# Experts: the next tokens' transposes ahead of a slice's gate product, and the down weights' split in two

## What is computed

```
scores = softmax(x @ W_router)
topk_vals, topk_idx = top_k(scores, 2)
h = silu(einsum('td,edh->eth', xf, We_gate)) * einsum('td,edh->eth', xf, We_up)
y_all = einsum('eth,ehd->etd', h, We_down)
routed = einsum('etd,te->td', y_all, combine)
```

## Time and profile before

| | us |
|---|---|
| median of 3 runs | 1090.07 (1089.99 to 1092.28) |
| the profiled execution | 1088.47 |
| its span, first to last instruction | 1086.8 |
| TensorE busy | 1016.1 (93%) |
| TensorE weight loads busy | 858.2 (79%) |
| VectorE busy | 666.1 (61%) |
| ScalarE busy | 456.7 (42%) |
| GpSimd busy | 275.8 (25%) |

### The profile page before, as it was taken

The page is one execution under the profiler, slowest core; times in us unless marked ns, Lnnn a source line. Parts: engine busy times, 40 slices in busy tenths (PEclk is TensorE's granted clock), DMA queues, the critical chain, the costliest instruction groups (busy, mean ns, idle before and its releaser), DMA issues. The chain is left out here.

```text
span 1086.8 us, 18081 instructions
## 1 busy us (share of the span) xinstructions
PE 1016.1 (93%) x6368; PEld 858.2 (79%) x6368; DVE 666.1 (61%) x1502; ACT 456.7 (42%) x798; POOL 275.8 (25%) x367
## 2 busy tenths in 40 slices
PE   7899999999979999999859979999999999899997
PEld 5688888888778888887637768888998889778785
DVE  4836556477265776776444847776777776253576
ACT  5623314145125544454443226555655664221110
POOL 4510100213143323333343122212231220503040
PEclk9999999999978999999998979999999999999999
DMA  5403032023877888884432157787778773615042
GB/s 168 180 1 116 0 115 87 0 81 126 205 187 194 212 228 239 218 219 131 171 99 81 63 179 225 252 256 266 243 246 277 251 244 113 213 40 188 6 155 77
DMA packets 87183, 172.66 MB, mean 159 GB/s; under 512 B 8112, under 2 KB 36016, under 8 KB 85328
## 3 DMA queue, kind: packets, MB, share of 16 engines
q1 hardware_dynamic: 81008, 150.08, 44.6%
q0 software_dynamic: 6112, 21.76, 6.1%
HBM read 130.92 MB, written 37.49 MB: 155 GB/s over the span
## 5 line engine op out<-in xcount | busy, mean ns | idle before, releaser
L45 PE MATMUL e_ps_h<-e_x_lo,e_gu_hi 128*128 128x256 f32 (+1 forms) x384 | 111.3, 290 | 10.8 <-DVE e_x_lo L2141 8.7
L45 PE MATMUL a_ps_proj<-region_a_rounded,arena 128*128 128x512 f32 x272 | 107.4, 395 | 11.2 <-DVE region_a_rounded L369 6.2
L953 DVE CUSTOM_DVE_ANT_0 b_dump<-b_ps_s,b_mask 128x128 f32<-128x128 f32 (+1 forms) x256 | 80.4, 354 | 46.5 <-PE b_ps_s L1143 43.3
L47 PE MATMUL e_ps_h<-e_x_hi,e_gu_hi 128*128 128x256 f32 (+1 forms) x384 | 108.2, 282 | 0.0
L46 PE MATMUL e_ps_h<-e_x_hi,e_gu_lo 128*128 128x256 f32 (+1 forms) x384 | 108.2, 282 | 0.0
L46 PE MATMUL a_ps_proj<-region_a_rounded,arena 128*128 128x512 f32 x272 | 106.4, 391 | 0.0
L47 PE MATMUL a_ps_proj<-region_a_rounded,arena 128*128 128x512 f32 x272 | 106.4, 391 | 0.0
L2147 DVE TENSOR_TENSOR e_gu_lo<-f_region_a,e_gu_hi 128x704 fp32r<-128x704 f32 x92 | 81.3, 889 | 26.8 <-ACT e_gu_hi L2057 26.3
L388 DVE SCALAR_TENSOR_TENSOR f_region_b<-a_ps_proj,a_taps,f_region_b 128x510 f32<-128x510 f32 (+2 forms) x96 | 71.7, 746 | 40.8 <-ACT f_region_b L328 38.5
L843 ACT ACTIVATE b_pt<-b_ps_x 128x384 f32<-128x384 f32 x128 | 61.8, 487 | 61.2 <-PE b_ps_x L1167 61.1
L757 POOL TENSOR_SCALAR_AFFINE_SELECT b_pt<-b_pt 128x256 f32<-128x256 f32 x128 | 51.8, 407 | 122.6 <-ACT b_pt L843 121.9
(11 more groups left out here) (400 smaller groups left out, 2693.7 us busy)
## 6 DMA issues: line engine op xcount, KB each, us to landing
f_region_a<-we_gate_up SPq DMA_DIRECT2D x88, 352.0 KB, 5.6
qk_split<-arena SPq DMA_DIRECT2D x24, 512.0 KB, 5.8
y_slots<-f_region_b SPq DMA_DIRECT2D x16, 512.0 KB, 3.4
f_x_next<-x SPq DMA_DIRECT2D x7, 1024.0 KB, 7.1
b_sk<-qk_split SPq DMA_DIRECT2D x24, 256.0 KB, 4.4
b_sq<-qk_split SPq DMA_DIRECT2D x24, 256.0 KB, 5.7
f_region_a<-we_down SPq DMA_DIRECT2D x12, 512.0 KB, 4.0
f_region_b<-we_down SPq DMA_DIRECT2D x11, 512.0 KB, 4.0
```

The lines of the kernel that those rows point to most:

```text
L45: pe.matmul(out, a_hi, b_lo, start=first, stop=False)
L47: return pe.matmul(out, a_hi, b_hi, start=False, stop=last)
L953: ins = dve.tensor_tensor_reduce(dump[:, n % 2, cols], ps_s[:, n % 2, cols], mask[:, cols], -1.0, 3e38, ALU.add, ALU.min, peak[:, u, k, i: ...
```

## The change

TensorE: in a small tile `turn(m, k + 1)` stands ahead of both products of the slice, not between them. ScalarE and VectorE: the next tile's tokens are split at the second tile's end, behind its output copy; the third part of the next tile's gate and up moves behind them. In the small tile the first third of the down weights (unit 0) is split at the start, ahead of the fourth part, and the other two thirds after the silu (ScalarE) or after the small hidden product (VectorE). Nothing that SP and POOL do is reordered.

```diff
-            def split_down(m, k):
-                act.wait_ge(dn_loaded[k % 2], 32 * (SPAN * m + (k + 1) // 2))
-                act.wait_ge(y_ready, count(m, k, BLOCKS, 1))
-                act.activation(dn_hi[:], dn_raw[k % 2], ACT.Copy).then_inc(dn_hi_done, 1)
+            def split_down(m, k, units=slice(0, U)):
+                if units.start == 0:
+                    act.wait_ge(dn_loaded[k % 2], 32 * (SPAN * m + (k + 1) // 2))
+                    act.wait_ge(y_ready, count(m, k, BLOCKS, 1))
+                act.activation(dn_hi[:, units], dn_raw[k % 2][:, units], ACT.Copy).then_inc(dn_hi_done, 1)
@@ ScalarE, large_tile
                 if k % SPAN == 1:
-                    for c in range(3):
-                        split_gate_up(m, k + 2, c)
+                    split_gate_up(m, k + 2, 0)
+                    split_gate_up(m, k + 2, 1)
                 output(m, k)
+                if k % SPAN == 1:
+                    split_x(m, k + 2)
+                    split_gate_up(m, k + 2, 2)
@@ ScalarE, small_tile
-                split_down(m, k)
+                split_down(m, k, slice(0, 1))
                 split_gate_up(m, k + 1, 3)
                 act.wait_ge(h_ready, U * number(m, k) + 1)
                 act.activation(small_sg, bank(0), ACT.Silu).then_inc(silu_done, 1)
-                split_x(m, k + 1)
+                split_down(m, k, slice(1, U))
                 act.wait_ge(h_ready, U * number(m, k) + 3)
@@ VectorE
-            def split_down(m, k):
-                dve.wait_ge(dn_hi_done, number(m, k) + 1)
-                dve.tensor_tensor(dn_lo[:], dn_raw[k % 2], dn_hi[:].bitcast(F32), ALU.subtract).then_inc(dn_lo_done, 1)
+            def split_down(m, k, units=slice(0, U)):
+                dve.wait_ge(dn_hi_done, count(m, k, 1, 2) + (1 if units.start == 0 else 2))
+                ins = dve.tensor_tensor(dn_lo[:, units], dn_raw[k % 2][:, units], dn_hi[:, units].bitcast(F32), ALU.subtract)
+                if units.stop == U:
+                    ins.then_inc(dn_lo_done, 1)
@@ VectorE, large_tile: as ScalarE's
@@ TensorE, small_tile
+                turn(m, k + 1)
                 small_hidden(m, k, 0)
-                turn(m, k + 1)
                 small_hidden(m, k, 1)
```

## The result

| | before | after |
|---|---|---|
| median of the timed runs, us | 1089.01 (1084.41 to 1095.32, 16 runs) | 1083.32 (1079.34 to 1088.36, 16 runs) |
| ratio of the times, 95% interval | | 0.9946 [0.9927, 0.9965] |
| profiled execution, us | 1088.47 | 1080.20 |
| its span, us | 1086.8 | 1078.4 |

The interval stands for 3.8 to 7.9 us, so rival (a) with its 7.5 us lies inside it too; (b), (c), (d) and (e) lie outside. A second set of runs gave 0.9943 [0.9915, 0.997]. Single executions lie up to 11 us apart before and 9 us after, so one profiled pair doesn't measure the gain: its spans differ by 8.4 us.

A forecast was written before the change was run, and what follows sets the result against it. TensorE bounds the kernel, with 9.4 us of waits at seven small tiles set by ScalarE's order and the third part. Place gains of 5.8, rounded to 5.7, gave 1090.07 - 5.7 = 1084.4 us; range 1081.5 to 1088.0 (8 in 10).

The forecast's parts named there:

- (a): Rival, chance 0.10: ScalarE's chain is shorter, TensorE's queue sets all restarts but for gathers; gain 7.5 us, 1082.6 us.
- (b): Rival, chance 0.11: later store and earlier gather each cost 0.5 us in seven places; 2.2 us gain left, 1087.9.
- (c): Rival: gate and up loads land at fixed times, only the first place gains; 1089.0 us; chance 0.09 together with (e).
- (d): Rival, chance 0.06: TensorE stands at later-landing gathers ahead of both products; 2.2 us later each loses 6.0 us, 1096.1 us.
- (e): Rival: no effect, something else comes last at the same moment; 1090 us; chance 0.09 together with (c).
- The chain of before: ScalarE's output copy through down weights, fourth part, silu and tokens to TensorE's restart: 4.34 us, setting all seven restarts.
- The new chain: ScalarE, from the second gate and up part's end to TensorE's restart: 4.07 us, 0.96 shorter than the 5.03 before.
- Gain by place: TensorE's seven small-tile restarts: 1.07, 1.1, 1.0, 0.4, 0.2, 1.0 and 1.0 us gained, together 5.8.
- The pauses: TensorE waiting for the gather before the moved transposes: 0.65 us at place 1, at most 0.7 each, 1.9 in all.
- VectorE's 0.1 in four places: Places 1, 3, 6, 7: VectorE's rest of the fourth part comes 0.1 to 0.2 us late; 0.1 taken off each.
- The queues: SP's later second-tile store and POOL's earlier gather: costed at nothing, at most 0.5 us a place each without cover.
- The signs that it named: Wrong if waits move to the gather, ScalarE's steps to the silu exceed 4.1 us, or down products begin to wait.

The follow-up runs named there:

- the kernel with all three: The changed kernel plus store before the third part's load, transposes half by half, and VectorE's product between the token halves: 1074.30 us against 1086.87, ratio 0.9896.

## Why the prediction held, step by step

**What bounds the kernel, and the chain.** The chain of before held, and the length of the new one too; how often the new one sets a restart did not (see the next part). Before, the copy-to-restart distance is 4.29 to 4.35 in fourteen of fourteen places of two traces, and it moves by 0.85 when the down weights are split, with the transposes in either order. The new chain is seen whole at the third place of the changed kernel, where it sets the restart:

```profile
743.56 0.58 ACT L2078 ACTIVATE f_region_b<-e_ps_y 128x512 f32<-128x512 f32 x1
744.04 1.07 ACT L2051 ACTIVATE e_x_hi<-e_ps_x 128x512 fp32r<-128x512 f32 x2
744.99 0.80 ACT L2057 ACTIVATE e_gu_hi<-f_region_a 128x704 fp32r<-128x704 f32 x1
745.67 0.64 ACT L2063 ACTIVATE e_dn_hi<-f_region_a 128x512 fp32r<-128x512 f32 x1
746.20 0.80 ACT L2057 ACTIVATE e_gu_hi<-f_region_a 128x704 fp32r<-128x704 f32 x1
746.88 0.47 ACT L2108 ACTIVATE f_region_b<-e_ps_h 128x352 f32<-128x352 f32 x1
```

From start to start: copy 0.48, tokens 0.95, part 0.68, third of the down weights 0.53, part 0.68, then the silu's 0.47 and 0.23 to TensorE's restart at 747.58. That is 4.02 where I had 4.07. The tokens were 0.13 cheaper than 2 x 0.54, since a step to the next instruction is shorter than a duration, and the last hop 0.07 dearer. The third of the down weights had no row and was put at 0.53: it is 0.53. The Trainium skill (VectorE: DVE Perf Modes, section "The TRN2 errata") gives ScalarE 224 cycles and one for each column when it reads SBUF, where the down weights are, and 172 and one for each column when it reads PSUM. An estimate by its row for SBUF is (224 + 512)/1.2 ns, 0.61 us for 512 columns. The trace has a duration of 0.64 and a step of 0.53, and the step is what a chain pays. For the 512-column copies from PSUM the table's estimate of 0.57 us meets a duration of 0.58 and a step of 0.48. For float32 additions of two tensors on VectorE the same section of the Trainium skill has the formula (N + 151)/0.96 ns; taken for the subtractions here, it gives estimates of 0.69, 0.89, 1.22 and 1.76 us for 512, 704, 1024 and 1536 columns. The traces agree with 0.69, 0.88 to 0.89, 1.22 and 1.75.

**Gain by place.** What each place lost before to W, against W and P after, from the first trace of each:

| place | 1 | 2 | 3 | 4 | 5 | 6 | 7 | sum |
|---|---|---|---|---|---|---|---|---|
| lost before | 1.72 | 1.42 | 2.41 | 0.44 | 0.16 | 1.44 | 1.82 | 9.4 |
| lost after | 0.95 | 0.96 | 0.69 | 0 | 0 | 0 | 0.42 | 3.0 |
| gained | 0.77 | 0.46 | 1.72 | 0.44 | 0.16 | 1.44 | 1.40 | 6.4 |
| forecast | 1.07 | 1.1 | 1.0 | 0.4 | 0.2 | 1.0 | 1.0 | 5.8 |

The forecast took this trace's landings of before as they were. In places 3 and 6 the second part's split started 0.5 us sooner in relation to TensorE than before, and in places 1 and 2 the gather landed 0.3 and 0.6 later than put down. These are landings, which differ from one execution to the next by such amounts. The sum was right to 0.6, single places to no better than 0.7. One thing is more than scatter. The forecast let the new chain set the restarts of places 3, 6 and 7, with 2.7 us lost there in all. Measured are 1.1 us in this trace and 0.45 in the second, nearly all of it pauses; the chain sets a late restart only at the third place of the first trace (0.18 us) and the first of the second (0.13). So in its windows the changed kernel is the one of rival (a), whose restarts all follow TensorE's queue, and the windows of 4.72 to 4.92 us lie at the lower end of the announced 4.8 to 5.8 or below it.

**The pauses.** Forecast 0.65, 0.3, 0.3, 0, 0, 0.2 and 0.4, 1.9 in sum. Measured 0.91, 0.92, 0.51, 0, 0, 0, 0.38 (2.7) and 0.31, 0.09, 0.40, 0, 0, 0, 0 (0.8). Their mean is 1.8. The mechanism, the size of the sum and the two places without any were right. The announced bound of 0.7 us for a single pause was not: two are 0.91 and 0.92.

**VectorE's 0.1 in four places.** The rest of the fourth part was ready in time at the first place (677.83, needed at 678.19), and TensorE waited once in the stretch for such a rest, 0.4 us, at 641.39, ahead of all small tiles. This term should have been 0, and nothing hangs on it; only in the kernel with all three does such a rest end the wait of a small tile, 0.35 us at the third place.

**The queues: the term that was mis-sized.** I put the later store at nothing, since it would be a few tenths late in three places and VectorE's copy and the product behind it had more than a microsecond to spare. Two steps of this failed. The landing was priced at 3.4 us, the median of all sixteen such stores, but the seven stores that count, those of the second tiles, took 4.7 to 5.5 us in the trace of before already, and 4.5 to 6.4 in the second trace of the change. And there was no microsecond to spare. The next down product of the small tile doesn't suffer, but the first tile of the next group does, whose product waited for e_h_lo before as well: eight such waits with 3.6 us stood in the trace of before, in a view of which the prediction used one line. So nearly all of the 1.3 and 2.0 us by which the copies are late reaches TensorE: H rose by 1.1 and 2.0. That lies inside the bound of 0.5 us a place, but the forecast had it at nothing. It was made up by a W + P that fell more than forecast (by 6.4 and, in the second trace, 8.4 against 5.8). That the two errors nearly cancel, so that 5.7 was forecast and 5.7 measured, is luck; what the prediction knew was the size, to about a microsecond or two.

**The signs that it named.** The waits did move in part to the gather (P), as the forecast itself had it. ScalarE's steps stayed under the 4.1 us (4.02 with the hop to TensorE). The down products, which had waited before, wait longer, and by the prediction's own words that is a sign against it: it points at the one term that was wrong, the queues.

**What part does the work.** The prediction summed one chain for the whole diff and never priced its pieces apart, though its numbers could have said it. From the end of the second part it is 5.03 before and 4.07 with everything; with the split alone it is 5.03 - 0.85 = 4.18. Measured: 0.70 and 3.49, so 4.19, and 4.02 with everything. Moving the tokens ahead of the third part takes the landing of that part out of the chain, which brings W from 3.2 to 0.2 or 0.3. It costs P (0.8 to 2.7) and H (1.6 to 2.6 more than with the split alone). The two sides cancel, and the split alone measures 0.9935 against 0.9943 and 0.9946. The reverse isn't shown: everything without the split measures 0.9951 [0.9926, 0.9977], which the times don't tell from the change either. Against it speak its chain, 0.85 us longer, and its stretch of 285.1 in one execution. So the split is shown to be enough for the gain, and not shown to be the only way to it. The statement that the old order wouldn't have used earlier transposes held as a mechanism (4.34 unchanged); that the same kernel's stretch came out 1.8 us shorter is open.

**The rivals.** (a), a shorter chain that leaves the queue to set all restarts, has the windows of both traces right, though not its reason: the chain is as long as forecast, and it starts early enough. H kept its 7.5 us from coming out, and the interval doesn't exclude them. (b) was right that the moved store costs; that the earlier gather costs anything, no run shows. Its 2.2 us of gain lie outside the interval. (c), loads at fixed times, falls with its gain of 1.1 us; and ScalarE's waits for them went from 12.1 to 8.8 us in the stretch, where they would have grown. (d) is a mechanism that exists. Its sum counted in landings, and in the kernel with the gathers held back the seven second halves landed 9.7 us later in all than in the change (the mean of its two traces); less the 3.7 of slack that is 6.0, and the stretch rose by 5.7. That is close, though the pauses alone rose by 7.4 and H and the rest fell by about 2. Its condition, later landings, didn't occur in the change beyond the scatter: measured from the point where a window could start, the seven landings sum to +0.4 and -1.9 us in its two traces and to -0.7 and -1.1 in those of before. (e) falls by the interval.

## What to carry to other kernels

Where a chain of one engine's instructions sets a restart, look first for a long instruction in it whose result is wanted in pieces, and split that one: here 1024 columns moved behind the silu were enough for the gain, and a reordering across three engines on top of it gave nothing that could be measured. Price the parts of a diff one by one, each with what it newly waits for. Price a transfer by its own issues at that place in the trace, not by the median of all like it (4.7 to 5.5 us against 3.4 here). Before writing that it costs nothing when later, follow the waiting engine's queue to the next wait of the bounding engine that already exists, even a tile further on; such a wait has no slack at all, and here it was the better thing to mend (one product moved took the stretch from 281.0 to 277.3 us).

## What the runs showed of the hardware

- Landings of the same load in the same kernel scatter more than the effects sought: two traces of the kernel before had the third window at 7.15 and 5.98 us with an identical chain of 4.34 behind the landings, and in two traces of the change the gather's pauses summed to 2.7 and 0.8 us. The chain of the engines' own steps repeats to 0.01 us in the first six places of both traces of before (4.34 and 4.35).
- The first gather instruction of a pair takes POOL 1.53 to 1.54 us in the regular places of every trace but the one where it is held back, where it takes 0.99. The change's own rows for the first place, to set beside those of the held-back kernel:

```profile
662.86 1.54 POOL L2028 DMA_INDIRECT f_region_b<-x,e_index  x1
664.70 0.95 POOL L2028 DMA_INDIRECT f_region_b<-x,e_index  x1 [0.30 <-issue]
```

  Between the starts it is 1.84 us against 1.29. So the same instruction of POOL takes longer or shorter with the moment at which it runs; on what that depends, no run here separates. With it, the first half held back by 2.6 us means the second held back by 2.0.
- Holding the gathers back took all of ScalarE's waits for gate and up weights away (8.8 us to none), and the gathers' own time to landing fell a little (median of all 6.0 and 5.7 us, mean at the seven places 6.7 and 6.4 against 5.9). That the loads profit from gathers issued later is the likely reading; TensorE's pauses gave them time as well, and no run separates the two.
